# Who splits the hidden layer, and in which order SyncE serves a tile: a gated cross-attention block with a mixture of experts

## The chip, the cores and the metric

The kernel runs on one core of one Trainium2 chip. The metric is the device time of one execution in microseconds (us). The kernel before took 954.37 us (median of three runs, 951.24 to 958.21).

## The reference, cut to what matters

`x` is 16 batches of 256 tokens with 512 features. It goes through cross-attention, and then through a mixture of 8 experts with three layers each:

```python
x = x + tanh(g_xattn) * xattn(layernorm(x), ctx, Wq, Wkv)
x = x + tanh(g_ffn) * ffn(layernorm(x), ...)

def ffn(x):                                   # B=16, S=256, D=512, E=8, K=2
    probs = softmax(x @ gate_w + gate_b, axis=1)
    vals, idx = top_k(probs, 2)
    h = relu(x @ w1[e] + b1[e])
    h = relu(h @ w2[e] + b2[e])
    y = relu(h @ w3[e] + b3[e])
    v[e] = sum over tokens of y * w_tok       # weight 0 for tokens that did not choose e
    out = ind @ v                             # ind: which experts a token chose
```

Only the chosen pairs of token and expert count, so the kernel computes 8192 rows, not 8 x 4096.

## The kernel before, in words

Every product of float32 values is made of three matmuls: each operand is split into a high part (rounded to the matmul type) and a low part (the rest), and `split_product` (L1314) sums high x high, high x low and low x high (lines 1319, 1320, 1321). So every operand needs two passes over its data before TensorE may read it: one that writes the high part, one that subtracts it.

The first part (about 0 to 330 us) does the attention batch by batch, chooses two experts for each token, and writes (token, weight) pairs into lists per expert in DRAM (`send_pairs`). The second part (330 to 925 us) cuts these lists into tiles of 352 rows; there are 24 here. A tile m has three layers, of 48 matmuls each. The last part (from 925 us) adds each expert's vector to the rows.

One tile passes through these steps:

- SyncE's queue: `load_idx` (L485) loads the row numbers, `load_w(n)` (L450) the weights of layer n (only where the tile has another expert than the tile before; w1, which is n=0, in four pieces at L463, the others at L457), `load_b` (L475) the bias, `load_wb` (L492) the token weights.
- POOL: `gather` (L651) fetches the 352 rows into `xg` by three indirect DMAs (L664). It may start when `idx` has landed and, from tile 5 on, when the rows of the tile before have left `xg`.
- SyncE's queue, from tile 4 on: `store_rows` (L525) sends `xg` to `rows_dram` (L531, L532), and `load_quarters` (L534) brings it back as `xq` in four DMAs (L541), in a layout that DVE transposes in blocks of 32. Tiles 0 to 3 are transposed by TensorE (`row_transposes`, L1535).
- DVE: `transpose_blocks` (L1192) makes `et`; ACT's `et_high` (L844) and DVE's `et_low` (L1198) split it.
- ACT `split_w` (L822) and DVE `w_low` (L1180) split the weights, 128x2048 each.
- TensorE runs layer 1 (`layer1_half`), ACT's `relu_half` (L827) writes `h` from the banks, two instructions of 128x352 for each half (L836). DVE's `h_high` (L1184) casts a half to `h_hi` (L1190, 128x704), POOL's `h_low` (L668) subtracts it to `h_lo` (L674, 128x704). Layer 2 reads both, then the same again, then layer 3.
- DVE's `weighted_sum` (L1208) reduces layer 3's banks with the token weights to `part` (L1226), and adds it to the expert's sum.

All of `h` is one buffer: `relu_half` waits until `h_lo` of its other use is written. Layer 1 of a tile reuses the banks of layer 3, so it waits for `part_done` of the tile before the previous one (L1493).

The order on each engine is written out by hand. TensorE runs, in its tile j: layer 2 of j, layer 1 of j+1, layer 3 of j. The function `tile(j, left)` of each engine gives the rest, with `left` cutting off what does not exist at the end:

- SyncE (L543): w3 and b2 of j+1; w2 and b1 of j+2; w1 of j+3, `store_rows(j+3)`; b3 and wb of j+1 (these wait for `part_done` of tile j); `load_quarters(j+3)`; `load_idx(j+4)`.
- POOL (L698): `h_low(1, j)`, `h_low(0, j+1)`, `gather(j+3)`.
- ACT (L880): `split_w(2, j)`, `relu(1, j)`, `split_w(1, j+1)`, `relu(0, j+1)`, `split_w(0, j+2)`, `et_high(j+2)`.
- DVE (L1271): `w_low(2, j)`, `h_high(1, j)`, `w_low(1, j+1)`, `h_high(0, j+1)`, `transpose_blocks(j+2)`, `w_low(0, j+2)`, `et_low(j+2)`, `weighted_sum(j)`.

Tiles 0 and 1 overlap with the end of the attention part, in an order of their own (DVE L1236 to L1269, ACT L856 to L878, POOL L684 to L696). There, `h_high(0, 0)` stands ahead of `two_best(B-2)` on DVE, and TensorE's `ranks(B-2)` (L1379) waits for `two_best`.

Of the kernel before, what the change touches and what calls it, by code (L numbers as in the profile page):

```python
# [19 lines left out]
DC = D // P  # L20
# [72 lines left out]
def has_tile(ahead, left):  # L93

    return ahead < left


def flamingo_block(nc, x, x_t, ctx_t, g_xattn, g_ffn, wq_t, wk_t, wv, gate_w, gate_b,
# [15 lines left out]
    with ExitStack() as ctx:  # L114
# [287 lines left out]
        def _(sp):  # L402
# [72 lines left out]
            def load_b(n, m):  # L475
                if n < 2:
                    need(sp, relu_done[n], DC * m)
                else:
                    need(sp, part_done, m)
                wait_alone(sp, "sp")  # L480
                e = sp.value_load(table[0:1, bass.ds(m, 1), 0:1], min_val=0, max_val=E - 1)
                sp.dma_start(bias[n][:], b_dram[n][bass.ds(e, 1)].rearrange("a p c -> (a p) c")
                             ).then_inc(b_in[n], 16)

            def load_idx(m):  # L485
                need(sp, gathered, 16 * TH * m)
                wait_alone(sp, "sp")
                r = sp.value_load(table[0:1, bass.ds(m, 1), 1:2], min_val=0, max_val=NSLOT - TILE)
                for c, (first, rows) in enumerate(CHUNKS):
                    sp.dma_start(idx[0:rows, c], slot_pair[bass.ds(r + first, rows)]).then_inc(idx_in, 16)  # L490
# [52 lines left out]
            def tile(j, left):  # L543
                if has_tile(1, left):
                    load_w(2, j + 1)
                    load_b(1, j + 1)
                if has_tile(2, left):
                    load_w(1, j + 2)
                    load_b(0, j + 2)
                if has_tile(3, left):  # L550
                    load_w(0, j + 3)
                    if not isinstance(j, int):
                        store_rows(j + 3)
                if has_tile(1, left):
                    load_b(2, j + 1)
                    load_wb(j + 1)
                if has_tile(3, left) and not isinstance(j, int):
                    load_quarters(j + 3)
                if has_tile(4, left):
                    load_idx(j + 4)  # L560

            tile(0, AHEAD + 1)
            tile(1, AHEAD + 1)
# [16 lines left out]
        def _(pool):  # L580
# [115 lines left out]
            gather(4)  # L696

            def tile(j, left):  # L698
                if has_tile(0, left):
                    h_low(1, j)  # L700
                if has_tile(1, left):
                    h_low(0, j + 1)
                if has_tile(3, left):
                    gather(j + 3)

# [11 lines left out]
        def _(act):  # L717
# [109 lines left out]
            def relu_half(n, m, k):  # L827


                act.wait_ge(l_done[n], 2 * m + k + 1)  # L830
                if n == 0:
                    need(act, h_los[1], 2 * (m - 1) + k + 1)
                else:
                    need(act, h_los[0], 2 * m + k + 1)
                for oc in range(2 * k, 2 * k + 2):
                    act.activation(h[:, oc], layer_banks(n, m)[oc][:, 0:TILE], ACT.Relu,  # L836
                                   bias=bias[n][:, oc:oc + 1]).then_inc(relu_done[n], 1)

            def relu(n, m):
                act.wait_ge(b_in[n], 16 * (m + 1))  # L840
# [63 lines left out]
        def _(dve):  # L904
# [276 lines left out]
                dve.wait_ge(w_his[n], m + 1)  # L1181
                low(w_lo[n][:], w_raw[n][:], w_hi[n][:], w_los[n])

            def h_high(n, m):  # L1184
                need(dve, l_done[n + 1], 2 * m)
                if n == 1 and isinstance(m, int) and m == 0:
                    dve.wait_ge(gate_done, B)
                for k in range(2):
                    dve.wait_ge(relu_done[n], DC * m + 2 * k + 2)
                    dve.tensor_copy(h_hi[n][:, 2 * k:2 * k + 2], h[:, 2 * k:2 * k + 2]).then_inc(h_his[n], 1)  # L1190

            def transpose_blocks(m):  # L1192
                dve.wait_ge(xq_in, 16 * NQ * (m - BY_BLOCKS + 1))
# [11 lines left out]
                    low(et_lo[:, :, a:a + n], row_banks(m)[c][:, 0:DC * n].rearrange("p (c s) -> p c s", c=DC),  # L1205
                        et_hi[:, :, a:a + n], et_los)

            def weighted_sum(m, last=False):  # L1208

                dve.wait_ge(b_in[2], 16 * (m + 1))  # L1210
                dve.wait_ge(wb_in, 16 * (m + 1))
                dve.tensor_scalar(nb3[:], bias[2][:], -1.0, None, ALU.mult).then_inc(wsum_step, 1)
                dve.tensor_reduce(wsum[:], wb[:, :, 1], AX_X, ALU.add).then_inc(wsum_step, 1)
                dve.wait_ge(wsum_step, 2 * m + 2)
                for oc in range(DC):
                    if last:
                        dve.wait_ge(last_done, oc + 1)
                    elif oc % 2 == 0:
                        dve.wait_ge(l_done[2], 2 * m + oc // 2 + 1)
                    z = layer_banks(2, m)[oc][:, 0:TILE]  # L1220
                    dve.scalar_tensor_tensor(out=z, in0=z, scalar=nb3[:, oc:oc + 1], in1=wb[:, :, 1],
                                             op0=ALU.max, op1=ALU.mult,
                                             accum_out=acc[:, oc:oc + 1]).then_inc(tail_small, 1)
                    dve.wait_ge(tail_small, DC * m + oc + 1)
                need(dve, v_acc, 2 * m)
                dve.scalar_tensor_tensor(out=part[:], in0=bias[2][:], scalar=wsum[:, 0:1], in1=acc[:],  # L1226
                                         op0=ALU.mult, op1=ALU.add).then_inc(part_done, 1)
                dve.wait_ge(part_done, m + 1)
                dve.tensor_tensor(v_add[:], part[:].unsqueeze(1).broadcast_to([P, E, DC]),
                                  tile_onehot[:, :, bass.ds(m, 1)].broadcast_to([P, E, DC]), ALU.mult  # L1230
                                  ).then_inc(v_acc, 1)
                dve.wait_ge(v_acc, 2 * m + 1)
                dve.tensor_tensor(v_sum[:], v_sum[:], v_add[:], ALU.add).then_inc(v_acc, 1)
# [9 lines left out]
            gate_softmax(B - 2)  # L1243
            attended(B - 1)
            w_low(1, 0)
            h_high(0, 0)
            two_best(B - 2)
            et_low(1)
            gt_low(B - 1)
            slots(B - 2, (B - 2) % 2)  # L1250
            w_low(0, 1)
            gate_softmax(B - 1)
            h_high(1, 0)
            w_low(2, 0)
            two_best(B - 1)
            h_high(0, 1)
            w_low(1, 1)
            slots(B - 1, (B - 1) % 2)
            w_low(0, 2)
            et_low(2)  # L1260
            weighted_sum(0)
            w_low(2, 1)
            h_high(1, 1)
            full_table()
            w_low(1, 2)
            h_high(0, 2)
            w_low(0, 3)
            et_low(3)
            weighted_sum(1)  # L1269

            def tile(j, left):  # L1271
                if has_tile(0, left):
                    w_low(2, j)
                    h_high(1, j)
                if has_tile(1, left):
                    w_low(1, j + 1)
                    h_high(0, j + 1)
                if has_tile(2, left):
                    if not isinstance(j, int):
                        transpose_blocks(j + 2)  # L1280
                    w_low(0, j + 2)
                    et_low(j + 2)
                if has_tile(0, left):
                    weighted_sum(j, last=(left == 1))

            tiles = tiles_in_use(dve)
            tile_pipeline(dve, tile, tiles)
# [373 lines left out]
```

## Time and profile before

| | us |
|---|---|
| median of three runs | 954.37 |
| lowest, highest | 951.24, 958.21 |
| the profiled execution, its own time | 953.95 |
| its span, first to last instruction | 952.2 |

The span is 1.75 us shorter than the time of the same execution. In the profile, "idle before <-X" is the time that an engine stood still ahead of an instruction, and what released it. PE is TensorE's matmul side; its granted clock is 1.00 at full speed (2.4 GHz) and 0.50 at half (1.2 GHz). Lines L12 are lines of the kernel.

### The profile page before, as it was taken

To read this page: it belongs to the slowest core of one execution; us is meant where nothing else is said; L and a number is where in the kernel's file an instruction comes from. 1 tells how busy PE (TensorE), PEld (TensorE's weight loads), DVE (VectorE), ACT (ScalarE), POOL (GpSimd) and SP (SyncE) were. 2 spreads that over 40 slices of the span, in tenths; PEclk is the share of its full clock that TensorE was granted. 3 is DMA by queue.
4 is the path that set the end of the run, shared out by engine and by line. 5 is a ranking of instruction groups with operands and counts; after the bars stand their busy time and mean duration, and the time that the engine had idled before them with its cause. 6 is when DMAs were issued, how large, how long until landed. Compare 5 with 4: busy or idle time off the path is not lost.

```text
span 952.2 us, 18810 instructions
## 1 busy us (share of the span) xinstructions
PE 918.2 (96%) x5746; PEld 863.7 (91%) x5746; DVE 721.6 (76%) x1379; ACT 419.5 (44%) x594; POOL 454.7 (48%) x402
## 2 busy tenths in 40 slices
PE   9999999999999979999999999999999999999985
PEld 6989888899888869899999999999999999999981
DVE  5667787887888867876877786889877777777646
ACT  5454443544433455344444444444444444444311
POOL 4225444444434566653655453655544554455213
PEclk9999999999999998999999999999999999999995
DMA  6433322233211544446656777866565555564008
GB/s 233 155 114 110 130 91 88 93 127 115 106 66 67 143 128 84 135 90 184 184 165 172 208 215 221 239 222 184 133 173 158 150 154 148 150 185 119 17 16 352
DMA packets 91924, 138.67 MB, mean 146 GB/s; under 512 B 28528, under 2 KB 56944, under 8 KB 88688
## 3 DMA queue, kind: packets, MB, share of 16 engines
q1 hardware_dynamic: 84464, 120.86, 42.8%
q0 software_dynamic: 7424, 17.38, 6.2%
q8 instruction: 18, 0.29, 0.1%
q14 instruction: 18, 0.15, 0.1%
HBM read 106.66 MB, written 31.53 MB: 145 GB/s over the span
## 4 chain that ended last, share of the span: by engine, by line
PE 65%; issue 11%; POOL 7%; DVE 6%; DMA 5%; SPq 4%; ACT 1%; POOLq 0%; DVEq 0%; ACTq 0%
PE bank L1319 20%; PE bank L1320 19%; PE bank L1321 19%; POOL h_lo L674 4%; POOL xg L664 3%; DMA rows_dram<-xg 2%; DMA xg<-xn_dram,idx 2%; DVE x_all L1309 2%; PE bank L1333 1%; PE bank L1390 1%; SPq L541 1%; PE bank L1431 1%; DMA idx<-slot_pair 1%; SPq L463 1%; PE bank L1433 1%
## 5 line engine op out<-in xcount | busy, mean ns | idle before, releaser
L674 POOL TENSOR_TENSOR h_lo<-h,h_hi 128x704 fp32r<-128x704 f32 x96 | 183.6, 1916 | 245.2 <-DVE h_hi L1190 245.2
L1319 PE MATMUL bank<-h_hi,w_hi 128*128 128x352 f32 x752 | 245.7, 327 | 7.3 <-POOL h_lo L674 4.1
L1321 PE MATMUL bank<-h_hi,w_lo 128*128 128x352 f32 x752 | 243.6, 324 | 0.0
L1320 PE MATMUL bank<-h_lo,w_hi 128*128 128x352 f32 x752 | 242.6, 323 | 0.0
L930 DVE TENSOR_TENSOR w_lo<-w_raw,w_hi 128x2048 fp32r<-128x2048 f32 x72 | 181.0, 2514 | 22.4 <-ACT w_hi L825 18.0
L836 ACT ACTIVATE h<-bank,bias 128x352 f32<-128x352 f32 x192 | 95.8, 551 | 201.0 <-PE bank L1321 170.8
L825 ACT ACTIVATE w_hi<-w_raw 128x2048 fp32r<-128x2048 f32 x72 | 137.8, 1916 | 54.6 <-PE bank L1321 46.0
L1319 PEld LDWEIGHTS bank<-h_hi,w_hi 128*128 128x128 f32 x752 | 142.1, 189 | 9.6 <-issue 9.6
L1320 PEld LDWEIGHTS bank<-h_lo,w_hi 128*128 128x128 f32 x752 | 142.1, 189 | 0.0
L1321 PEld LDWEIGHTS bank<-h_hi,w_lo 128*128 128x128 f32 x752 | 141.7, 188 | 0.0
L1319 PE MATMUL bank<-et_hi,w_hi 128*128 128x352 f32 x384 | 125.0, 326 | 4.5 <-DVE part L1226 2.6
L1190 DVE CAST h_hi<-h 128x704 fp32r<-128x704 f32 x96 | 69.1, 725 | 76.3 <-ACT h L836 76.3
L1320 PE MATMUL bank<-et_lo,w_hi 128*128 128x352 f32 x384 | 123.7, 322 | 0.0
L1321 PE MATMUL bank<-et_hi,w_lo 128*128 128x352 f32 x384 | 123.7, 322 | 0.0
L664 POOL DMA_INDIRECT xg<-xn_dram,idx x72 | 104.5, 1452 | 36.6 <-issue 16.6
L634 POOL DMA_INDIRECT slot_pair<-pair,slot_u x64 | 66.1, 1033 | 36.5 <-DVE pair L987 19.3
L1319 PEld LDWEIGHTS bank<-et_hi,w_hi 128*128 128x128 f32 x384 | 72.5, 189 | 5.5 <-issue 3.1
L1320 PEld LDWEIGHTS bank<-et_lo,w_hi 128*128 128x128 f32 x384 | 72.7, 189 | 0.0
L1321 PEld LDWEIGHTS bank<-et_hi,w_lo 128*128 128x128 f32 x384 | 72.6, 189 | 0.0
L601 POOL TENSOR_SCALAR rn<-mv 128x2 f32<-128x2 f32 x32 | 9.4, 293 | 131.1 <-DVE mv L927 131.1
L1319 PE MATMUL bank<-xt_hi,a_hi 128*128 128x256 f32 x240 | 69.1, 288 | 0.0
L1195 DVE STREAM_TRANSPOSE et<-xq 128x1408 f32<-128x1408 f32 x20 | 54.8, 2739 | 17.5 <-DMA xq<-rows_dram 17.4
(202 smaller groups left out, 1767.1 us busy)
## 6 DMA issues: line engine op xcount, KB each, us to landing
w_raw<-in_w SPq DMA_DIRECT2D x24, 1024.0 KB, 5.1
xq<-rows_dram SPq DMA_DIRECT2D x80, 176.0 KB, 4.1
w_raw<-in_w SPq DMA_DIRECT2D x48, 256.0 KB, 6.1
rows_dram<-xg SPq DMA_DIRECT2D x20, 512.0 KB, 3.1
wb<-slot_pair SPq DMA_DIRECT2D x24, 352.0 KB, 4.1
xt_raw<-in_x_t SPq DMA_DIRECT2D x16, 512.0 KB, 3.9
c_raw<-in_ctx_t SPq DMA_DIRECT2D x16, 512.0 KB, 3.3
x_all<-in_x SPq DMA_DIRECT2D x16, 512.0 KB, 4.8
```

The source lines that it names most:

```text
L634: pool.indirect_dma_start(slot_pair, bass.IndirectOffsetOnAxis(ap=slot_u[:, k, n:n + 1], axis=0), pair[:, k, n], None).then_inc(pair_sent[ ...
L664: pool.indirect_dma_start(xg[0:n, c], None, rows, bass.IndirectOffsetOnAxis(ap=idx[0:n, c, 0:1], axis=0)).then_inc(gathered, 16)
L674: pool.tensor_tensor(h_lo[n][:, 2 * k:2 * k + 2], h[:, 2 * k:2 * k + 2], h_hi[n][:, 2 * k:2 * k + 2].bitcast(F32), ALU.subtract).then_inc( ...
L825: act.activation(w_hi[n][:], w_raw[n][:], ACT.Copy).then_inc(w_his[n], 1)
L836: act.activation(h[:, oc], layer_banks(n, m)[oc][:, 0:TILE], ACT.Relu, bias=bias[n][:, oc:oc + 1]).then_inc(relu_done[n], 1)
L930: dve.tensor_tensor(dst, src, hi.bitcast(F32), ALU.subtract).then_inc(done, 1)
L1190: dve.tensor_copy(h_hi[n][:, 2 * k:2 * k + 2], h[:, 2 * k:2 * k + 2]).then_inc(h_his[n], 1)
L1195: dve.transpose(et[:].rearrange("p k (g b) -> p g k b", b=QB), xq[:].rearrange("p g (i k) -> p g k i", k=DC)).then_inc(et_ready, 1)
L1309: dve.tensor_tensor(row, bank[n % 8][:], row, ALU.add).then_inc(res_dve, 1)
L1319: pe.matmul(out_ap, lh, rh, start=(i == 0), stop=False)
L1320: pe.matmul(out_ap, lh, rl, start=False, stop=False)
L1321: last = pe.matmul(out_ap, ll, rh, start=False, stop=(i == n - 1))
```

## The change

ACT's `relu_half` gets the high part: behind its two relus it waits for them and for the readers of `h_hi`, and copies the half to `h_hi`. DVE's `h_high` goes; in the loop of tiles DVE gets `h_rest`, which subtracts the low part, in the places that `h_high` had. In POOL's loop only `gather` is left; ahead of the loop (tiles 0 and 1, and layer 1 of tile 2) POOL still writes the low part, from ACT's high part. In SyncE's tile, `store_rows(j+3)`, `load_idx(j+4)` and `load_quarters(j+3)` are issued ahead of w1 of j+3 and of b3 and wb of j+1. The two small instructions of `weighted_sum` that read only the bias and the token weights become `weights_of` and move ahead of `w_low(0, j+2)`.

```diff
@@ sync: tile(j, left)
                 if has_tile(2, left):
                     load_w(1, j + 2)
                     load_b(0, j + 2)
+                if has_tile(3, left) and not isinstance(j, int):
+                    store_rows(j + 3)
+                if has_tile(4, left):
+                    load_idx(j + 4)
                 if has_tile(3, left):
+                    if not isinstance(j, int):
+                        load_quarters(j + 3)
                     load_w(0, j + 3)
-                    if not isinstance(j, int):
-                        store_rows(j + 3)
                 if has_tile(1, left):
                     load_b(2, j + 1)
                     load_wb(j + 1)
-                if has_tile(3, left) and not isinstance(j, int):
-                    load_quarters(j + 3)
-                if has_tile(4, left):
-                    load_idx(j + 4)
@@ gpsimd: tile(j, left)
-                if has_tile(0, left):
-                    h_low(1, j)
-                if has_tile(1, left):
-                    h_low(0, j + 1)
                 if has_tile(3, left):
                     gather(j + 3)
@@ scalar: relu_half(n, m, k)
                 for oc in range(2 * k, 2 * k + 2):
                     act.activation(h[:, oc], layer_banks(n, m)[oc][:, 0:TILE], ACT.Relu,
                                    bias=bias[n][:, oc:oc + 1]).then_inc(relu_done[n], 1)
+                need(act, l_done[n + 1], 2 * m)
+                if n == 1 and isinstance(m, int) and m == 0:
+                    act.wait_ge(gate_done, B)
+                act.wait_ge(relu_done[n], DC * m + 2 * k + 2)
+                act.activation(h_hi[n][:, 2 * k:2 * k + 2], h[:, 2 * k:2 * k + 2], ACT.Copy).then_inc(h_his[n], 1)
@@ vector
-            def h_high(n, m):
...
+            def h_rest(n, m):
+                for k in range(2):
+                    dve.wait_ge(h_his[n], 2 * m + k + 1)
+                    low(h_lo[n][:, 2 * k:2 * k + 2], h[:, 2 * k:2 * k + 2], h_hi[n][:, 2 * k:2 * k + 2], h_los[n])
+
+            def weights_of(m):
                 dve.wait_ge(b_in[2], 16 * (m + 1))
                 dve.wait_ge(wb_in, 16 * (m + 1))
                 dve.tensor_scalar(nb3[:], bias[2][:], -1.0, None, ALU.mult).then_inc(wsum_step, 1)
                 dve.tensor_reduce(wsum[:], wb[:, :, 1], AX_X, ALU.add).then_inc(wsum_step, 1)
+
+            def weighted_sum(m, last=False):
...
@@ vector, ahead of the loop: the five h_high calls go, weights_of(0) and weights_of(1) stand ahead of weighted_sum
@@ vector: tile(j, left)
                 if has_tile(0, left):
                     w_low(2, j)
-                    h_high(1, j)
+                    h_rest(1, j)
                 if has_tile(1, left):
                     w_low(1, j + 1)
-                    h_high(0, j + 1)
+                    h_rest(0, j + 1)
                 if has_tile(2, left):
                     if not isinstance(j, int):
                         transpose_blocks(j + 2)
+                weights_of(j)
+                if has_tile(2, left):
                     w_low(0, j + 2)
                     et_low(j + 2)
-                if has_tile(0, left):
-                    weighted_sum(j, last=(left == 1))
+                weighted_sum(j, last=(left == 1))
```

## Rows read from the trace of the kernel before

**Rows 1.** The page: span, busy time of each engine.
```profile
span 952.2 us, 18810 instructions
PE 918.2 (96%) x5746; PEld 863.7 (91%) x5746; DVE 721.6 (76%) x1379; ACT 419.5 (44%) x594; POOL 454.7 (48%) x402
```

**Rows 2.** Windows of one tile late in the loop (columns: PE, PEld, DVE, ACT, POOL, clock, DMA).
```profile
700.00:723.06 23.06, 23.06 (x146) 23.06 (x145) 17.36 (x23) 10.92 (x12) 11.45 (x8) 1.00 0.67 197
```

**Rows 3.** Waits of PE from 350 to 925 us (total, times, longest).
```profile
PE bank L1319 <- POOL h_lo L674: 4.1, 4, 1.4
PE bank L1319 <- DVE part L1226: 2.6, 2, 1.3
PE bank L1379 <- DVE ind L1053: 2.6, 1, 2.6
PE bank L1319 <- issue: 1.9, 2, 1.1
```

**Rows 4.** Timeline around 593 to 600 us: DVE, POOL and PE.
```profile
593.76 3.79 DVE L930 TENSOR_TENSOR w_lo<-w_raw,w_hi 128x2048 fp32r<-128x2048 f32 x1
593.50 5.60 POOL L674 TENSOR_TENSOR h_lo<-h,h_hi 128x704 fp32r<-128x704 f32 x2 [7.89 <-DVE h_hi L1190]
599.34 0.42 PE L1319 MATMUL bank<-h_hi,w_hi 128*128 128x352 f32 x1 [1.38 <-POOL h_lo L674]
```

**Rows 5.** Waits of DVE, 430 to 930 us (total, times, longest).
```profile
DVE et L1195 <- DMA xq<-rows_dram: 17.4, 7, 5.0
```

**Rows 6.** SyncE's queue: timeline, 560 to 577 us; one of its waits, 405 to 930 us.
```profile
560.34 2.92 SPq L463 DMA_DIRECT2D w_raw<-in_w  x4
568.76 0.40 SPq L531 DMA_DIRECT2D rows_dram<-xg  x1
574.59 1.86 SPq L541 DMA_DIRECT2D xq<-rows_dram  x4
SPq L384 <- DMA xg<-xn_dram,idx: 46.9, 16, 5.3
```

**Rows 7.** Groups by form, 700 to 792 us (four tiles): DVE, ACT, POOL.
```profile
L930 DVE TENSOR_TENSOR w_lo<-w_raw,w_hi 128x2048 fp32r<-128x2048 f32 x12 | 29.6, 2463 | 5.1 <-ACT w_hi L825 4.4 <-issue 0.8
L1190 DVE CAST h_hi<-h 128x704 fp32r<-128x704 f32 x16 | 9.1, 570 | 16.0 <-ACT h L836 16.0
L1201 DVE TENSOR_TENSOR et_lo<-et,et_hi 128x1408 fp32r<-128x1408 f32 x5 | 8.1, 1617 | 0.0
L825 ACT ACTIVATE w_hi<-w_raw 128x2048 fp32r<-128x2048 f32 x12 | 23.0, 1916 | 8.4 <-PE bank L1321 8.4
L848 ACT ACTIVATE et_hi<-et 128x1408 fp32r<-128x1408 f32 x4 | 5.5, 1387 | 6.1 <-DVE et L1195 6.1
L674 POOL TENSOR_TENSOR h_lo<-h,h_hi 128x704 fp32r<-128x704 f32 x16 | 27.4, 1711 | 43.4 <-DVE h_hi L1190 43.4
```

**Rows 8.** Timeline, 605 to 609 us: two gather DMAs of one tile on POOL.
```profile
604.70 0.97 POOL L664 DMA_INDIRECT xg<-xn_dram,idx  x1 [1.26 <-DMA idx<-slot_pair]
605.97 3.06 POOL L664 DMA_INDIRECT xg<-xn_dram,idx  x1 [0.30 <-issue]
```

**Rows 9.** Timeline around 727 to 731 us: DVE's sum, PE's next layer 1.
```profile
727.36 0.22 DVE L1226 SCALAR_TENSOR_TENSOR part<-bias,wsum,acc 128x4 f32<-128x4 f32 x1
731.28 0.32 PE L1319 MATMUL bank<-et_hi,w_hi 128*128 128x352 f32 x1
```

**Rows 10.** Timeline, 353 to 359 us: ACT, DVE, POOL, PE.
```profile
353.85 0.97 ACT L836 ACTIVATE h<-bank,bias 128x352 f32<-128x352 f32 x2
354.85 0.53 DVE L1190 CAST h_hi<-h 128x704 fp32r<-128x704 f32 x1 [4.03 <-ACT h L836]
355.46 1.67 POOL L674 TENSOR_TENSOR h_lo<-h,h_hi 128x704 fp32r<-128x704 f32 x1 [1.44 <-DVE h_hi L1190]
358.15 0.66 PE L1319 MATMUL bank<-h_hi,w_hi 128*128 128x352 f32 x1
```

**Rows 11.** A window behind that wait, PE alone (busy, count, clock, DMA).
```profile
358.00:362.00 4.00, 4.00 (x15) 0.50 0.57 160
```

More of the change, by code:

```diff
@@ L1182, in w_low @@
                 low(w_lo[n][:], w_raw[n][:], w_hi[n][:], w_los[n])
-            def h_high(n, m):
[L1185 to L1190, printed above, removed]
             def transpose_blocks(m):
@@ L1206, in et_low @@
                         et_hi[:, :, a:a + n], et_los)
-            def weighted_sum(m, last=False):
+            def h_rest(n, m):
[3 more added lines that the diff above has]
+            def weights_of(m):
                 dve.wait_ge(b_in[2], 16 * (m + 1))
@@ L1245, in _ @@
             w_low(1, 0)
-            h_high(0, 0)
             two_best(B - 2)
@@ L1252, in _ @@
             gate_softmax(B - 1)
-            h_high(1, 0)
             w_low(2, 0)
             two_best(B - 1)
-            h_high(0, 1)
             w_low(1, 1)
@@ L1260, in _ @@
             et_low(2)
+            weights_of(0)
             weighted_sum(0)
             w_low(2, 1)
-            h_high(1, 1)
             full_table()
             w_low(1, 2)
-            h_high(0, 2)
             w_low(0, 3)
             et_low(3)
+            weights_of(1)
             weighted_sum(1)
```

## The prediction, made before the changed kernel was run

> **What bounds the kernel now.** I read the page first: TensorE is busy 96% of a span of 952.2 us, every other engine well below [rows 1]. Its busy time includes matmuls of the same count and size after the change, so the only thing to win is the time in which it stands still or runs at half clock. Windows of one tile show where that is not: at 700 us a tile of 23.06 us has 23.06 us of PE at clock 1.00, 146 instructions of PE, DVE 17.36, ACT 10.92, POOL 11.45 [rows 2]. That stretch cannot gain, only lose. PE's own waits show where something is left [rows 3]: between 350 and 925 us it stood 4.1 us, four times, until POOL's `h_lo` was there, 2.6 us, twice, until DVE's `part` was there, 2.6 us once for `ind` (the choice of experts), and 1.9 us, twice, with "issue", which is a wait whose releaser the profile doesn't show. By their places in the timeline the first six lie at 447, 456, 550, 590, 599 and 646 us, all in the first half of the loop.
>
> Why there? Rows 4 show one. DVE's `w_lo` took 3.79 us, while POOL's two `h_lo` took 5.60 us together, against 1.71 us each [rows 7]; PE stood 1.38 us until they were done. DVE was late before it got there: it waited 17.4 us in all, seven times and up to 5.0 us, for `xq`, the quarters of the gathered rows [rows 5]. And SyncE's queue says why these were late: the w1 pieces went out at 560.34, the rows only at 568.76 and the quarters at 574.59 [rows 6], because the gather, which POOL starts behind its `h_low` of the tile, had not landed: waits for it sum to 46.9 us on SyncE, 16 times [rows 6]. So the chain is gather, rows, quarters, transpose, and then a burst of late DVE work that collides with POOL's.
>
> **The loop, part by part.** POOL loses four `h_low` of 1.71 us for each tile, 6.8 us, and the wait for DVE ahead of them, so that the gather can start as soon as its numbers are there and `xg` is free, some 10 us earlier. SyncE issues rows, numbers and quarters when w2 and b1 are out: 2 + 3 + 4 DMAs, about 5 us of its queue with their waits. From the w1 issue at 560.34 to the end of the quarters' at 576.45 it was 16.1 us [rows 6]; the quarters now no longer wait for w1 nor for `part_done`. DVE asks for them a whole tile later, so the 17.4 us of waiting should go, except for tile 4, the first that uses quarters.
>
> ACT gains four copies of 128x704 per tile. Its copies of 2048 and 1408 elements take 1.916 and 1.387 us [rows 7]: 0.83 ns for an element, so 0.81 us for 704. ACT goes from 10.92 to 14.2 us of 23.06. Behind each copy on ACT stand the next weight split or relu, and both have room: ACT idles 8.4 us for w in four tiles only because PE isn't ready [rows 7]. It also adds a wait of ACT for its own relu, some 0.1 us, 4 times.
>
> DVE loses four casts of 0.57 us and gains four subtractions of 128x704. The trace has none of that size on DVE. Low bound: the cast, 0.57 us; high bound: POOL's 1.71 us; nearest row: `et_lo`, twice as large, 1.62 us [rows 7], so with a fixed part 0.9 us. DVE comes to 17.36 + 4 x (0.9 - 0.57) = 18.7 us a tile, at the high bound 21.9 us. Even this is below 23.06. In return its `w_lo`, at 2.46 us on average and 3.79 in a collision [rows 4, 7], has no `h_lo` on POOL beside it any more.
>
> What is later in the steady tile: the last `h_lo` half on DVE comes 0.81 + 0.1 + 0.9 - 0.57 = 1.2 us later than the cast did, and everything behind it, to `part`, moves by that. `part` ended 3.7 us before layer 1 asked for it (727.58 to 731.28) [rows 9]; 2.5 us stay. For PE itself `h_lo` is earlier, 0.1 + 0.8 + 0.9 = 1.8 us behind the relu, against 0.57 + 1.71 = 2.3. So the steady tile stays at 23.06 us, and this part of the change costs nothing as long as PE covers it. `weights_of` is the same work a few us earlier.
>
> With the quarters in time, DVE runs in the early tiles as it does at 700 us, where PE never waits. So the four `h_lo` waits (4.1 us) and both `part` waits (2.6 us) go: **-6.7 us**. The first two of them (2.7 us, at 447 and 456 us) hang on tile 4, whose gather starts on POOL behind `h_low(0, 2)` as before, but without collisions; I count them as gone too.
>
> One rule of the Trainium skill speaks against the change, and the sum does without it. The row: a gather DMA of POOL took 3.06 us beside DVE's `w_lo`, where one took 0.97 us just before [rows 8]. SBUF — State Buffer (section "SBUF: two separate sides") says that DVE and GpSimd share a port pair as an exclusive lock, held for a whole instruction, which DVE also takes with two SBUF inputs against a GpSimd operation that reads SBUF. Rows 4 and 8 agree with a lock, and by it the new DVE subtractions are four more locks for the gathers to wait behind, where a cast was. That would stretch the gather by at most 4 x 0.9 us, which is less than the 6.8 us that POOL no longer spends; the sum is the same by rule and by row.
>
> **The transition (350 to 415 us).** At present DVE does `h_high(0, 0)` before it looks for the two best experts. It waited 4.03 us for ACT's relu, until 354.85 [rows 10], and PE's `ranks` waited 2.6 us for the outcome [rows 3]. Now DVE goes there at 350.8, and `ranks` stands ready. But layer 2 of tile 0 needs `h_lo` too: relu until 354.82, copy on ACT 0.8 us with its wait, POOL's 1.67 us [rows 10], gives 357.5 to 357.6 us, where PE started at 358.15. So of 2.6 us only **-0.55 us** come off; the next wait was right behind. Bounds: 0 and 1.0 us.
>
> PE's clock fell after that wait: 15 matmuls in the 4 us from 358.0, at 0.50 [rows 11], where a steady tile has 146 in 23.06, 25 in 4 us. At 1.2 GHz a matmul step was 0.29 us, at 2.4 GHz 0.16 us; it lasted to 363.3 us, 17 steps, so this fall cost 17 x 0.13 = 2.2 us. The idle stretch before it becomes shorter by 0.55 us of some 3 us. Whether that spares the fall is open: between 0 and 2.2 us, I take a third, **-0.7 us**.
>
> The two "issue" waits (1.9 us) [rows 3] stand at 389 us (0.8) and 415 us (1.1). The first ends with DVE's `et_lo` of tile 2; in front of it a small DVE operation took 0.58 instead of 0.19 us beside POOL's `h_lo`: **-0.4 us**. The second ended after `et_lo` of tile 3 and `h_lo` of tile 2, both held up by the collision of `w_lo` and `h_lo` (3.79 and 3.8 us). Both now come over 1 us earlier, but a register load of TensorE's stands in the same place; I take half, **-0.55 us**, with bounds 0 and 1.1.
>
> **Sum.** 953.95 - 6.7 - 0.55 - 0.7 - 0.4 - 0.55 = **945.1 us**. This is against the profiled execution's own time; the median, 954.37, lies 0.4 us above, and I leave the forecast there. It is 1.0% below the median, on the very limit of what a measurement of this kernel can tell from no change (about 1%).
>
> **Rivals.** (a) The quarters stay late in the dense stretch. For: between 460 and 620 us six w1 loads follow each other, together with w2 and w3, and single gathers landed after 10 us. Against: the queue gives them some 16 us more. Then the waits at 550, 590, 599 and 646 us stay, 0.9 + 1.3 + 1.4 + 0.4 = 4.0 us: 949.1 us. Chance 0.25.
>
> (b) Slower: w1 becomes the late one. It is now behind the rows, the quarters and all that they wait for. Its pieces went out at 560.34 and the last landed at 572.8, when ACT's split of it began at 574.26: 1.5 us to spare in the worst tile. Behind that split DVE and PE have about the 2.5 us of above. It decides when w1 goes out more than 4 us later than now; at 6.5 us later, each of the six loads of the dense stretch costs 2.5 us, and the other gains are as forecast: 945.1 + 15 = 960 us. Against: rows and quarters are ready earlier, so that they take only their issue time from it, and `w_low(0, j+2)` releases w1 no earlier than before. Chance 0.05.
>
> (c) The change does what it says, but the early waits were not due to the quarters, and all that is gone is the transition's: 951.7 us. Against: DVE's seven waits for `xq` lie exactly in these tiles. Chance 0.1.
>
> **Numbers.** Forecast 0.6, (a) 0.25, (b) 0.05, (c) 0.1. The forecast's own range, with the bounds of the transition (0 to 1.0 + 2.2 + 0.4 + 1.1 = 4.7 us, of which I took 2.2), is 942.6 to 947.3. With (a) and most of (c), and a little below for clock falls that differ from run to run, the range is 941.5 to 951.0. Faster by over 1% means below 944.8: a little under half, all from the forecast, 0.44. Slower by over 1%: 0.04, from (b). Within: 0.52.
>
> **What would show it.** In the changed profile: no PE wait for `h_lo` or `part` from 430 us on; DVE's wait for `xq` near zero but for tile 4; SyncE issuing the quarters ahead of w1 with no long wait for the gather; ACT near 14 and DVE near 18.7 us in a steady tile that still takes 23.06 us; DVE's `h_lo` at 0.9 us; and PE's start of layer 2 of tile 0 on POOL's `h_lo`, not on `ranks`. It is wrong if PE waits for `w_lo` behind a late w1 (then b), or if the steady tile grows.

## The result, and the profile after

| | before, us | after, us |
|---|---|---|
| median of 17 runs each, on one chip | 955.09 | 950.70 |
| lowest, highest | 951.24, 958.21 | 948.27, 953.51 |
| profiled execution: own time | 953.95 | 951.54 |
| its span | 952.2 | 949.8 |

The ratio is 0.9949, with a 95% interval of 0.9934 to 0.9964: by the medians 4.4 us gained, where 9.3 were forecast against the median of before (954.37). The sign and the range were right, the size was not.

The page after; its lines answer to [rows 1]:

```profile
span 949.8 us, 18798 instructions
PE 919.3 (97%) x5746; PEld 865.7 (91%) x5746; DVE 709.1 (75%) x1369; ACT 495.5 (52%) x690; POOL 273.3 (29%) x316
```

The work moved as the diff says: ACT 76 us more, POOL 181 us less. The window of one steady tile answers to [rows 2], and the groups by form, 700 to 792 us, to [rows 7]:

```profile
700.00:723.06 23.06, 23.06 (x146) 23.06 (x146) 17.98 (x23) 14.09 (x17) 3.75 (x4) 1.00 0.53 155
```
```profile
L931 DVE TENSOR_TENSOR w_lo<-w_raw,w_hi 128x2048 fp32r<-128x2048 f32 x12 | 27.5, 2290 | 4.4 <-ACT w_hi L821 3.7 <-issue 0.8
L664 POOL DMA_INDIRECT xg<-xn_dram,idx x12 | 14.9, 1240 | 77.3 <-DMA idx<-slot_pair 74.9 <-issue 2.4
L931 DVE TENSOR_TENSOR h_lo<-h,h_hi 128x704 fp32r<-128x704 f32 x16 | 14.2, 888 | 14.8 <-ACT h_hi L838 14.8
L838 ACT ACTIVATE h_hi<-h 128x704 fp32r<-128x704 f32 x16 | 12.7, 794 | 0.5
```

A tile still takes 23.06 us. DVE's subtraction is 888 ns (forecast 0.9 us), ACT's copy 794 ns (0.81), and `w_lo` is 173 ns shorter without POOL's `h_lo` beside it.

Waits of PE, 350 to 925 us, then DVE's for the quarters (430 to 930) and SyncE's for the gather (405 to 930); they answer to [rows 3, 5, 6]:

```profile
PE bank L1317 <- issue: 4.2, 2, 3.8
...
PE bank L1317 <- POOL h_lo L674: 2.2, 1, 2.2
DVE et L1189 <- DMA xq<-rows_dram: 6.5, 1, 6.5
SPq L384 <- DMA xg<-xn_dram,idx: 8.8, 1, 8.8
```

The waits named `part` and `ind` are gone, and so are the four for `h_lo` in the loop; the one for `h_lo` that is left is the new one at 360 us. But one stall of 3.8 us has come, with no releaser named. The timeline puts it at the start of layer 1 of tile 4, and the windows show half clock behind it (columns as in [rows 2]):

```profile
450.78 0.22 DVE L1226 SCALAR_TENSOR_TENSOR part<-bias,wsum,acc 128x4 f32<-128x4 f32 x1
451.15 0.40 PE L1317 MATMUL bank<-et_hi,w_hi 128*128 128x352 f32 x1 [3.78 <-issue]
```
```profile
452.00:456.00 4.00, 4.00 (x18) 4.00 (x17) 4.00 (x4) 0.42 (x1) 2.54 (x2) 0.57 0.77 196
456.00:460.00 4.00, 4.00 (x26) 4.00 (x26) 2.76 (x2) 1.79 (x3) 0.00 (x0) 1.00 0.76 212
```

`part` ended at 451.0 and PE went on 0.15 us later, so it is DVE's sum that PE waited for, though the row says "issue". It is the sum of tile 2, which layer 1 of tile 4 needs; on DVE it stands behind the transpose, `w_low` and `et_low` of tile 4. PE runs layer 1 of a tile, then layer 3 of the tile before, then layer 2 of the tile itself. Setting the starts of the layers of both traces side by side gives the whole account:

| stretch, by starts of layers | before | after | change | forecast |
|---|---|---|---|---|
| start to layer 1 of tile 0 | 341.87 | 345.52 | +3.65 | 0 |
| to layer 3 of tile 2 (transition) | 88.51 | 86.25 | -2.26 | -2.2 |
| to layer 3 of tile 3 (around layer 1 of tile 4) | 26.17 | 28.73 | +2.56 | -2.7 |
| to layer 3 of tile 13 (dense stretch) | 236.24 | 230.57 | -5.67 | -4.0 |
| to the end of the span | 259.39 | 258.70 | -0.69 | 0 |

They sum to -2.4 us, as the spans do. The first row is no part of the change (see the last section); without it this execution gained 6.1 us. The third row holds the two waits of before at 447 and 456 us: the first grew by 2.5 us, and the second (1.39 us for `h_lo`) went, but the half clock behind the longer stall cost as much, so that layer 1 of tile 4 takes 9.35 us, where it took 9.28. The last row is not explained; this stretch takes 258.7 to 259.3 us in the traces of the other kernels.

SyncE's queue says why tile 4 got worse; timeline of the changed kernel:

```profile
419.91 1.40 SPq L490 DMA_DIRECT2D idx<-slot_pair  x3
422.82 3.33 SPq L463 DMA_DIRECT2D w_raw<-in_w  x4
...
428.38 0.34 SPq L496 DMA_DIRECT2D wb<-slot_pair  x1
429.66 0.39 SPq L531 DMA_DIRECT2D rows_dram<-xg  x1
434.05 1.86 SPq L541 DMA_DIRECT2D xq<-rows_dram  x4
```

and the same queue before:

```profile
413.53 2.92 SPq L463 DMA_DIRECT2D w_raw<-in_w  x4
...
419.26 0.34 SPq L496 DMA_DIRECT2D wb<-slot_pair  x1
425.69 1.47 SPq L490 DMA_DIRECT2D idx<-slot_pair  x3
428.12 0.40 SPq L531 DMA_DIRECT2D rows_dram<-xg  x1
...
431.88 1.85 SPq L541 DMA_DIRECT2D xq<-rows_dram  x4
```

Before, w1 of tile 4 and b3 and wb of tile 2, all in SyncE's `tile(1)`, were issued while the gather of tile 4 was still on its way. Now `load_idx(5)` stands in front of them and waits 8.8 us for that gather; and as tile 4's rows and quarters are issued behind `tile(1)`, outside of the new order, they wait for all of it. The rows could have gone at 419.9 us and went at 429.7. Since the whole trace is later from the start on, the places are best read against PE, that is from its start of layer 3 of tile 2 (two kernels of the experiments are set beside them):

| us from layer 3 of tile 2 | before | after | split_only | rows4_first |
|---|---|---|---|---|
| numbers of tile 5, which wait for gather 4 | -4.7 | -11.9 | -7.8 | -10.1 |
| rows of tile 4 | -2.3 | -2.1 | -5.5 | -12.4 |
| quarters of tile 4 | +1.5 | +2.3 | -1.9 | -8.5 |
| DVE's transpose of them | +6.7 | +9.5 | +4.6 | +2.9 |

The gather landed some 7 us earlier than before, and the rows behind it no earlier: w1, b3 and wb, now queued behind the wait, used it up. The rows then take 4.4 us to the issue of the quarters, where they took 3.8, and the quarters 7.2 us from issue to transpose instead of 5.2. What runs beside the quarters is the gather of tile 5, which POOL now issues as soon as the rows have left `xg`, 0.67 us behind the first quarter; before, it stood behind two `h_lo` and was issued 2.2 us behind it (434.08 us):

```profile
434.72 0.96 POOL L664 DMA_INDIRECT xg<-xn_dram,idx  x1 [17.91 <-DMA rows_dram<-xg]
```

Such an early gather goes with slow quarters in after_again (7.0 us), split_only (6.4) and w1_ahead_at_start (6.3) too; no run takes it away alone. Together DVE's transpose is 2.7 us later against PE, and the stall of this place grew by 2.5 us (3.78 for 1.29 us).

### The profile page after: what moved, and what is told of

Its sections match the earlier page's. It is cut to its first block, busy times and chain, and to the rows that moved or that the text cites. A ratio compares the mean times of both kernels' runs of the same rounds, so it can differ in the third digit from the quotient of the medians.

```text
span 949.8 us, 18798 instructions
## 1 busy us (share of the span) xinstructions
PE 919.3 (97%) x5746; PEld 865.7 (91%) x5746; DVE 709.1 (75%) x1369; ACT 495.5 (52%) x690; POOL 273.3 (29%) x316
## 4 chain that ended last, share of the span: by engine, by line
PE 84%; DVE 5%; issue 3%; POOL 2%; DMA 2%; SPq 1%; ACT 1%; another core or an unknown queue 0%; DVEq 0%; POOLq 0%; ACTq 0%
PE bank L1317 26%; PE bank L1318 26%; PE bank L1319 26%; DVE x_all L1307 2%; PE bank L1331 1%; POOL h_lo L674 1%; PE bank L1388 1%; PE bank L1429 1%; DMA xq<-rows_dram 1%; PE bank L1431 1%; POOL xg L664 1%; POOL slot_pair L634 0%; DMA rows_dram<-xg 0%; PE bank L1351 0%; DMA wq_raw<-in_wq_t 0%
## 5 line engine op out<-in xcount | busy, mean ns | idle before, releaser
L664 POOL DMA_INDIRECT xg<-xn_dram,idx x72 | 88.5, 1229 | 371.6 <-DMA idx<-slot_pair 325.5
L931 DVE TENSOR_TENSOR w_lo<-w_raw,w_hi 128x2048 fp32r<-128x2048 f32 x72 | 164.8, 2289 | 27.4 <-ACT w_hi L821 23.0
L931 DVE TENSOR_TENSOR h_lo<-h,h_hi 128x704 fp32r<-128x704 f32 x86 | 76.3, 888 | 84.5 <-ACT h_hi L838 84.4
L838 ACT ACTIVATE h_hi<-h 128x704 fp32r<-128x704 f32 x96 | 76.3, 794 | 3.9
L1319 PE MATMUL bank<-xt_hi,a_lo 128*128 128x256 f32 x240 | 67.9, 283 | 0.0
L1318 PE MATMUL bank<-xt_lo,a_hi 128*128 128x256 f32 x240 | 67.9, 283 | 0.0
```

Of the source, the lines that this page charges most:

```text
L664: pool.indirect_dma_start(xg[0:n, c], None, rows, bass.IndirectOffsetOnAxis(ap=idx[0:n, c, 0:1], axis=0)).then_inc(gathered, 16)
L838: act.activation(h_hi[n][:, 2 * k:2 * k + 2], h[:, 2 * k:2 * k + 2], ACT.Copy).then_inc(h_his[n], 1)
L931: dve.tensor_tensor(dst, src, hi.bitcast(F32), ALU.subtract).then_inc(done, 1)
L1318: pe.matmul(out_ap, lh, rl, start=False, stop=False)
L1319: last = pe.matmul(out_ap, ll, rh, start=False, stop=(i == n - 1))
```

## The experiments

Twelve kernels were run in three batches, each on one chip. "Before" in a row is the kernel before on that chip.

| kernel | us | before | ratio, 95% interval |
|---|---|---|---|
| after_again | 947.50 | 950.33 | 0.9969 [0.9958, 0.9980] |
| rows4_first | 942.88 | 950.33 | 0.9918 [0.9899, 0.9937] |
| split_only | 942.92 | 950.33 | 0.9927 [0.9906, 0.9948] |
| sync_only | 957.45 | 950.33 | 1.0070 [1.0049, 1.0091] |
| w1_ahead_at_start | 945.65 | 952.18 | 0.9940 [0.9916, 0.9964] |
| high_on_act_alone | 944.54 | 952.18 | 0.9927 [0.9906, 0.9948] |
| low_on_dve_alone | 948.40 | 952.18 | 0.9962 [0.9943, 0.9981] |
| tile0_on_dve | 943.64 | 952.18 | 0.9910 [0.9885, 0.9935] |
| both_repairs | 945.35 | 954.96 | 0.9895 [0.9860, 0.9931] |
| rows4_first_again | 944.75 | 954.96 | 0.9893 [0.9858, 0.9927] |
| split_only_again | 947.02 | 954.96 | 0.9910 [0.9878, 0.9942] |
| after_third | 950.86 | 954.96 | 0.9955 [0.9935, 0.9976] |

**The changed kernel again** (no edit).

> The changed kernel once more, for a second trace. Theory A (the late semaphore of the last scores is an accident of one execution): in this trace DVE reads the last scores at once, PE's `ranks` wait at 331 us is 0.5 us and layer 1 of tile 0 starts near 342 us instead of 345.5; the span is then 946 to 948 us. Theory B (the change itself slows the attention part): DVE stands about 2 us there again and layer 1 starts at 345.5 us. Under both the stall ahead of layer 1 of tile 4 is there again, 3 to 4 us, since its quarters are issued behind w1 of tile 4.

Measured: 0.9969, layer 1 of tile 0 at 341.94 us as in the kernel before, and the stall at tile 4 in its place, 3.4 us with half clock from 447.13 to 450.55 us. The row, which this time names the releaser that the first trace did not (waits of PE, 350 to 925 us):

```profile
PE bank L1317 <- DVE part L1226: 3.4, 1, 3.4
```

So the 3.65 us were that execution's, and the stall at tile 4 is the kernel's.

**Tile 4's rows first.** In SyncE's `tile(1)`, tile 4's rows, the numbers of tile 5 and tile 4's quarters go ahead of w1:

```diff
+            def first_rows():
+                for n in range(NSEND):
+                    sp.wait_ge(pair_sent[n], 16 * RC * TOPK * sends_by_end(n))
+                store_rows(BY_BLOCKS)
+                load_idx(BY_BLOCKS + 1)
+                load_quarters(BY_BLOCKS)
@@ tile(j, left)
-                    load_idx(j + 4)
+                    if isinstance(j, int) and j + 4 == BY_BLOCKS + 1:
+                        first_rows()
+                    else:
+                        load_idx(j + 4)
@@ behind tile(1, AHEAD + 1)
-            (the same waits, store_rows(BY_BLOCKS), load_quarters(BY_BLOCKS))
```

> The changed kernel, but SyncE issues the rows, numbers and quarters of tile 4 ahead of w1 of tile 4 too. Theory A (the shortfall is the start of the loop): quarters go out 4 to 6 us earlier, DVE's wait of 6.5 us shrinks to under 1 us, PE's 3.8 us stall ahead of layer 1 of tile 4 goes and the half clock behind it (1.5 us) too: 5 us faster than the changed kernel, 945 to 946. Theory B (the quarters are late because gathers and w pieces collide in the queues, whatever their order): the quarters land within 1 to 2 us of where they did, gain 0 to 1.5 us.

Measured: 942.88 us, 4.6 less than the changed kernel on the same chip. Its queue on SyncE:

```profile
415.96 0.39 SPq L531 DMA_DIRECT2D rows_dram<-xg  x1
...
418.26 1.44 SPq L490 DMA_DIRECT2D idx<-slot_pair  x3
419.89 2.61 SPq L541 DMA_DIRECT2D xq<-rows_dram  x4
423.99 2.93 SPq L463 DMA_DIRECT2D w_raw<-in_w  x4
```

Its waits of DVE from 430 us on have no row for `xq`, its waits of PE none for `part`; the clock is 1.00 behind layer 1 of tile 4, which starts at 443.74 us. The `part` that this layer 1 needs ends 1.2 us ahead of it, and 2.72 to 2.75 us ahead in all 19 tiles behind it. The repeat:

> A repeat on the same chip as the others of this call: if the tile 4 order was the reason, some 4 us below the changed kernel here too, no wait of DVE for xq, slack ahead of layer 1 not below 1.2 us.

Measured: 944.75 us, 6.1 less than the changed kernel beside it (950.86), with the same slacks. That is 10.2 us, or 1.1%, below the kernel before on this chip, 7.4 us on the first.

> The changed kernel once more, as the level of this chip: 0.3 to 0.5% below the kernel before, with the stall of 3 to 4 us at layer 1 of tile 4 and the half clock behind it.

Measured: as expected (0.9955; 3.59 us of stall at 451.39, DVE's wait for `xq` 6.3 us).

**Each half of the change alone.** `split_only` is the changed kernel with SyncE's old order; `sync_only` the kernel before with SyncE's new order.

> The changed kernel with SyncE's old order: only ACT, DVE and POOL are changed. Theory A (the gather was late because POOL did h_low first; the order of SyncE is not needed): the waits at 550 to 646 us are gone as in the changed kernel, and the start of the loop is no worse than in the kernel before, since w1 of tile 4 goes out before the wait for the gather: 949 to 951 us, equal to the changed kernel or 1 us better. Theory B (both parts are needed): DVE waits again for quarters in the dense stretch, 3 to 4 us of PE stalls come back there, 953 us or more.

> The kernel before with SyncE's new order alone; POOL still writes h_lo ahead of each gather. Theory A (the gather is what is late): SyncE stands for the gather with w1 behind it, so quarters are no earlier by more than the 3 us of the w1 pieces and w1 is later: 953 to 960 us, no gain. Theory B (the order is what helps): the waits at 550 to 646 us go here too, and the time is 951 us.

Measured: the split of h alone is as fast as the repaired kernel (942.92), the new order alone costs 7 us. In the latter, the waits of PE, 350 to 925 us, hold the tile 4 stall (`part`, 4.5 us) and the old `h_lo` collisions, though DVE waits for the quarters only once:

```profile
PE bank L1319 <- DVE part L1226: 5.1, 2, 4.5
PE bank L1319 <- POOL h_lo L674: 4.2, 4, 1.4
DVE et L1195 <- DMA xq<-rows_dram: 8.2, 1, 8.2
```

So quarters in time were not enough. But this kernel has another input late in their place. ACT's waits for weights, 430 to 930 us, this kernel and then the one before:

```profile
ACT w_hi L825 <- DMA w_raw<-in_w: 49.2, 15, 5.5
```
```profile
ACT w_hi L825 <- DMA w_raw<-in_w: 8.6, 5, 2.2
```

By their places in ACT's timeline nine of the fifteen are for w1 (33 us), and of the five before none: w1, now queued behind waits for the gather of up to 9.6 us, is late, and with it DVE's `w_lo`. This kernel therefore does not refute that late quarters caused the waits of before; it shows that SyncE's new order needs a gather that starts early.

**What in the split does it?** `high_on_act_alone` is `split_only` with POOL still writing the low part in the loop; `low_on_dve_alone` is the kernel before with DVE casting and subtracting in the loop, and POOL only gathering.

```diff
@@ high_on_act_alone, against split_only: gpsimd tile(j, left); DVE's two h_rest calls in tile go
+                if has_tile(0, left):
+                    h_low(1, j)
+                if has_tile(1, left):
+                    h_low(0, j + 1)
@@ low_on_dve_alone, against before: POOL's two h_low calls in tile go; on DVE, behind each cast:
+                    dve.wait_ge(h_his[n], 2 * m + k + 1)
+                    low(h_lo[n][:, 2 * k:2 * k + 2], h[:, 2 * k:2 * k + 2], h_hi[n][:, 2 * k:2 * k + 2], h_los[n])
```

> Half of split_only: ACT writes the high part, POOL still writes the low part ahead of its gather in the loop; SyncE in the old order. Theory A (what counts is POOL's freedom to gather early): DVE still waits for quarters, about 15 us in all, but loses four casts a tile, so part of PE's loop stalls stays: 2 to 4 us slower than split_only. Theory B (what counts is DVE's time and the chain from relu to h_hi): stalls gone, equal to split_only within 1 us.

> The other half: from the loop on, DVE casts and subtracts, POOL only gathers, ACT as in the kernel before; SyncE in the old order. DVE then has 17.4 + 3.6 = 21 us of 23.06 in a tile. Theory A (POOL's freedom is what counts, DVE has the room): no stalls from 456 us on, 1.5 to 3 us slower than split_only because the transition keeps the waits for ind (0.6), et_lo and the register load (1.5). Theory B (DVE is too full, or its part comes too late): PE waits for part or h_lo in many tiles, some 0.3 us in each of 20: 5 us or more slower than split_only.

Measured: 0.9927 with the high part alone, 0.9962 with the low part alone. The first is the telling one; its DVE and PE waits, and its steady tile:

```profile
DVE et L1193 <- DMA xq<-rows_dram: 84.3, 20, 7.4
PE bank L1319 <- DVE part L1230: 0.5, 2, 0.2
700.00:723.06 23.06, 23.06 (x146) 23.06 (x145) 14.68 (x18) 14.10 (x17) 12.64 (x8) 1.00 0.61 163
```

DVE waits 84.3 us for the quarters, five times as long as before [rows 5], and PE's named waits for it sum to 0.5 us. That is not quite all: at six places `part` ends only 0.15 us ahead of layer 1, and the steps there are longer by 1.9 us in all; the dense stretch takes 232.05 us, 1.4 more than in split_only (230.68) and 4.2 less than before. POOL is as full as before. So later quarters cost little here, and POOL need not be freed. Whether that is because DVE has room (14.68 us of work in 23.06) or because `h_hi` no longer stands behind `w_lo` in DVE's queue, no run separates. The second kernel shows another way: DVE is fuller (20.21 us in the steady tile), POOL has only its gathers, and behind tile 4 no stall is left either (230.61 us for the dense stretch); it keeps the transition's waits and, at tile 4, a stall of 3.3 us for `part` with half clock behind it.

**The two orders once more.**

> The split of h alone, SyncE's old order. If DVE's chain is what counts, it is level with the kernel that has tile 4's rows first (within 1.5 us), but with a slack of part near zero or single stalls between 460 and 650 us, where the new order has 2.7 us. If SyncE's new order in the loop is worth time by itself, it is over 2 us slower than that kernel.

Measured: 947.02 (943.73 to 948.57) against 944.75 (944.17 to 945.96) for the new order with tile 4 repaired: 2.3 us by the medians, with ranges that overlap, where the first chip showed none. The traces show no stall of either in the loop. What differs is the margin: with the old order `part` comes down to 0.82, 0.26 and 1.58 us ahead of layer 1 (603 to 650 us; 1.49, 0.98 and 1.54 in the repeat), with the new one it stays at 2.72 or more. At layer 1 of tile 4 it is 1.05 and 0.49 us with the old order, 1.23 and 1.15 with the new one. In `tile0_on_dve`, below, the old order does stall there. So the new order buys margin; a time of its own is not shown.

**w1 ahead of the numbers.** If only w1's place was wrong, it is enough to put it back in `tile(1)`:

```diff
+                if has_tile(3, left) and isinstance(j, int):
+                    load_w(0, j + 3)
                 if has_tile(4, left):
                     load_idx(j + 4)
```

> The changed kernel; only ahead of the loop SyncE issues w1 of tile 4 before it waits for the gather of tile 4 (as the kernel before did); the loop keeps the new order. Theory A (w1's 3.1 us of issue behind the gather's wait of 8.9 us is all that makes tile 4 late): the rows of tile 4 go out 3 to 4 us earlier, PE's stall ahead of layer 1 of tile 4 (3.4 us) and the half clock behind it go, 4 to 5 us faster than the changed kernel, the same as rows4_first. Theory B (the loop's new order contributes to the loss, or the early w1 slows the gather's landing as much as it saves): gain under 2 us.

Measured: 0.9940, 2.6 us of stall left at tile 4; the stretch around layer 1 of tile 4 takes 25.85 us, 28.25 in after_again and 23.03 in rows4_first. The timeline of POOL and SyncE shows that the early w1 holds the gather up:

```profile
411.45 2.90 SPq L463 DMA_DIRECT2D w_raw<-in_w  x4
412.43 0.92 POOL L665 DMA_INDIRECT xg<-xn_dram,idx  x1 [0.30 <-issue]
421.53 1.41 SPq L490 DMA_DIRECT2D idx<-slot_pair  x3
```

The same in after_again, where w1 comes later:

```profile
411.66 0.92 POOL L664 DMA_INDIRECT xg<-xn_dram,idx  x1 [0.30 <-issue]
415.72 1.40 SPq L490 DMA_DIRECT2D idx<-slot_pair  x3
```

From the end of the last gather's issue to the numbers, which wait for it, it is 8.2 us with w1's four loads of 256 KB in flight, 3.1 us without. And b3 and wb still stand between the wait for the gather and the rows, which go out 4.7 us behind the numbers. In split_only, where w1, b3 and wb all go ahead of that wait, there is no stall at tile 4 either, in two traces, although its gather takes 7.1 us from there in the first. (In tile0_on_dve, below, which has the same order, there is one of 1.6 us.) By these runs, what tile 4 needs is its rows and quarters close behind the wait, with none of w1, b3 and wb between. The Trainium skill, DMA: Bandwidth & Descriptors, section "Issuing engines are not separate DMA queues", says that DMAs of all engines run on the same 16 DMA engines. By that rule the gather shares them with w1, and the two numbers agree; no run here tells which of its transfers stood behind which.

**The low part of tile 0 on DVE.** POOL's `h_low(0, 0)` goes, DVE's `h_rest(0, 0)` comes behind `two_best(B - 2)`, in `split_only` and in `rows4_first`:

> split_only, and DVE instead of POOL writes the low part of layer 1 of tile 0, behind two_best. The wait for h_lo ahead of layer 2 of tile 0 was 2.2 us with POOL's 1.7 us in it. Theory A (that wait's chain is relu, copy, subtraction): DVE's 0.9 us makes it 0.8 us shorter, and TensorE's half clock behind it is as long or shorter; 0.8 to 2.5 us faster than split_only. Theory B (another input is late right behind, or DVE's delay of et_lo and slots gives it back): 0 to 0.4 us.

> The changed kernel with the rows, numbers and quarters of tile 4 ahead of w1 of tile 4 in SyncE's tile(1), and with the low part of h of tile 0, layer 1, on DVE behind two_best(B-2) instead of on POOL. If the two repairs act in places that do not touch each other, they add: about 0.8 us below the kernel with the first alone (layer 2 of tile 0 starts on h_lo 0.8 us earlier), and no stall from 430 us on. If DVE's own queue is the limit around 360 us, the 0.8 us are given back before layer 1 of tile 1.

Measured: layer 2 of tile 0 starts 14.5 us behind layer 1 instead of 15.3, in both. The rows of PE in both_repairs and in the changed kernel:

```profile
360.34 0.63 PE L1323 MATMUL bank<-h_hi,w_hi 128*128 128x352 f32 x1 [1.38 <-DVE h_lo L936]
```
```profile
360.81 0.63 PE L1317 MATMUL bank<-h_hi,w_hi 128*128 128x352 f32 x1 [2.21 <-POOL h_lo L674]
```

But the time does not follow: both_repairs is level with rows4_first_again (945.35 and 944.75). Its trace loses 2.6 us in the next step, layer 2 of tile 0 to layer 1 of tile 1 (11.26 us against 8.68), since the clock was at 0.50 there and at 1.00 in the other; and DVE, which waits 3.1 us for `wb` of tile 2 (`weights_of`, ahead of the sum that layer 1 of tile 4 needs), delays PE by 0.5 us. The window with the half clock:

```profile
360.00:364.00 4.00, 3.66 (x13) 3.69 (x13) 3.90 (x12) 4.00 (x6) 0.99 (x1) 0.50 0.92 320
```

rows4_first has that wait too, 1.4 us, without a stall. For `tile0_on_dve` there is no `split_only` on the same chip to set its time against. In its trace quarters came late in the dense stretch: DVE waited 19.1 us for them, seven times, and PE 4.6 us, four times, for `part`, the first of them at tile 4:

```profile
DVE et L1188 <- DMA xq<-rows_dram: 19.1, 7, 4.3
PE bank L1317 <- DVE part L1225: 4.6, 4, 1.6
```

This profiled execution took 946.81 us, the other five 942.03 to 943.70, so these stalls are not those of a usual execution; they show how thin the margin of the old order is.

## Why the prediction came out half right

**The step that failed** is the sentence on the waits at 447 and 456 us, that they hang on tile 4, "whose gather starts on POOL behind `h_low(0, 2)` as before, but without collisions; I count them as gone too". It was worth -2.7 us; the place gave +2.6 us. I had followed the new order only in the loop, where rows, numbers and quarters go ahead of w1 together. In `tile(1)` only the numbers move up, with their wait for the gather, and tile 4's rows and quarters stay behind everything. rows4_first removes that and gains 4.6 and 6.1 us on two chips, against 5.3 between my number and the measured one at this place. With it, the kernel stands 7.4 and 10.2 us below the one before: the forecast was 9.3.

**The loop behind tile 4**: forecast -4.0, measured -5.67 us. All stalls went; the surplus of 1.7 us lies in what my list of single waits left out, steps that were longer than 15.43 us (layer 3 with the layer 2 behind it) and 7.63 us (layer 1) around them (15.51 to 15.57 at five places, 7.92 and 8.19 at two) and the restart behind each stall (9.25 for 7.63 us at 599, with 1.38 us of waiting). The steady tile, the costs on ACT and DVE (17.98 us for 18.7, since `w_lo` is shorter), the slack of `part` (2.5 forecast, 2.75 measured) were right.

**Why** it went is only in part what I had written. Two ways out are shown, each enough behind tile 4: `h_hi` taken from DVE (high_on_act_alone), with quarters later than ever, and the low part taken from POOL (low_on_dve_alone), with DVE fuller. So neither earlier quarters nor a freed POOL was needed. That the late quarters caused the waits of before stays an argument from one trace: the one kernel that has them in time with the old split, sync_only, made w1 late instead.

**The transition** was right in its sum (-2.26 for -2.2) and off in the terms. `ind` to `h_lo`: -1.0 for -0.55; the chain from the end of the relu to layer 2 took 2.72 us, as forecast, but the relu itself ended 0.4 us earlier against layer 1. The wait at 360 us is 2.21 us on POOL's `h_lo`, as named. The "issue" waits: -1.34 at 415 us for -0.55, and -0.42 before it for -0.4. The clock, of which I took 0.7, fell all the same, and the two steps behind it are 0.55 us longer than before: 19 matmul steps of 0.25 to 0.4 us there, where the kernel before has 16. It differs from trace to trace: 14 in after_again, 8 in split_only, 17 in both_repairs, none in rows4_first_again.

**The lock** that the rule of the Trainium skill describes (SBUF — State Buffer, "SBUF: two separate sides") is seen in the changed kernel as well, ahead of the loop; DVE and POOL, 405 to 414 us:

```profile
405.40 2.29 DVE L931 TENSOR_TENSOR w_lo<-w_raw,w_hi 128x2048 fp32r<-128x2048 f32 x1
405.64 3.61 POOL L674 TENSOR_TENSOR h_lo<-h,h_hi 128x704 fp32r<-128x704 f32 x1 [2.01 <-ACT h_hi L838]
411.17 2.29 DVE L931 TENSOR_TENSOR w_lo<-w_raw,w_hi 128x2048 fp32r<-128x2048 f32 x1 [3.47 <-ACT w_hi L821]
411.27 3.05 POOL L664 DMA_INDIRECT xg<-xn_dram,idx  x1 [0.16 <-issue]
```

Whoever starts second pays: POOL's 1.71 us become 3.61, its gather's 0.97 become 3.05. The four more subtractions of DVE's, against which the rule spoke, did no harm: a gather in the steady tiles takes 1240 ns on average, where it took 1607 ns before.

**Rivals.** (a), quarters that stay late in the dense stretch, did not come: one wait for `xq`, at tile 4. (b), a late w1, did come in one place and in another form: w1 of tile 4 went out 7.9 us later than before against PE's layers, and what it delayed was the rows behind it in the queue, not its own split. As it was written, a late split behind a late w1, it is seen in sync_only, where POOL's gathers start as late as before. (c) is refuted in its price by -5.67 us in the dense stretch; its premise, that the early waits were not due to the quarters, stays open by what is said above.

Not tried: the change without `weights_of` moved up, which would show whether the wait for `wb` ahead of layer 1 of tile 4 is worth anything; nor, in the kernel before, the quarters moved ahead of b3 and wb with w1 left in its place, which would show what the late quarters cost by themselves.

## What to carry to other kernels

When a queue's order is changed in a loop, write out the order of the first iterations too, with what is issued between prologue and loop: a wait that moves ahead of independent transfers there costs all of them its whole length. And ask of a late input not how late it is but how much slack lies behind its consumer: here 84 us of DVE's waiting, in 20 tiles, cost PE about 2 us, and 6.5 us in one tile cost it 3.8.

## What the runs showed beyond that

The 3.65 us at the start. In the profiled execution after, the last matmul of a row of scores started at 325.07 us, and DVE, which needs it, stood until 328.51 with no instruction named; in after_again it went on at once. Rows of DVE, the changed kernel first:

```profile
328.51 0.69 DVE L939 TENSOR_REDUCE smax<-bank 128x2 f32<-128x512 f32 x1 [1.98 <-remote]
```
```profile
326.46 0.66 DVE L939 TENSOR_REDUCE smax<-bank 128x2 f32<-128x512 f32 x1
```

PE then waited 2.41 us for `ind`, and its clock fell. Five of the fourteen traces have this, always at the same instruction and with 1.8 to 2.4 us of idle time: the changed kernel's first one, and all four of the third batch; none of the first two batches has it, and of the changed kernel's three traces two have it. That points to the chip or the occasion rather than to the kernel, but does not show it. What holds the semaphore back stays open. The medians of the same kernels were 1.9 to 4.6 us higher in that batch than in the first, the kernel before among them, which fits. A comparison of two single traces should therefore be made by stretches.
